# A graph network on one Trainium2 core: the dense sum by source inside the second graph-attention pass, and the residual layer in two stages

## What is computed

```python
x = _layernorm(x + _L0_gnn_ref(x, edge_index, ...))   # two graph-attention passes (gat_conv)
x = _layernorm(x + _L1_gnn_ref(x, src, dst, edge_weight, ...))   # residual layer
x = _layernorm(x + _L2_gnn_ref(x, edge_index, ...))   # attention with queries, keys, values
x = _layernorm(x + _L3_gnn_ref(x, src, dst, ...))     # edge network with batch norms
```

```python
h = (x @ W).reshape(N, H, C)
e = leaky_relu(alpha_s[src] + alpha_d[dst], 0.2)
e_exp = exp(e - segment_max(e, dst)[dst])
alpha = e_exp / (segment_sum(e_exp, dst)[dst] + EPS)
out = segment_sum(h[src] * alpha[:, :, None], dst) + bias

feat_neigh = segment_sum(edge_val[:, None] * feat_in[edge_col], edge_row)
_branch(f, W, b, i): h = relu(f @ W.T + b); (h - mean) * scale_i * rsqrt(var + 1e-9) + offset_i
result = _branch(feat_in, W_self, b_self, 0) + _branch(feat_neigh, W_neigh, b_neigh, 1)
```

## Time and profile before

| what | us |
|---|---|
| three runs | 12797.11, 12800.82, 12800.6 |
| median | 12800.6 |
| profiled execution | 12812.41 |
| its span | 12810.4 |
| busy PE, DVE, ACT, POOL | 3639.8, 6552.3, 2402.6, 7622.7 |
| second pass, first to last unit | 2999 to 5448 |
| from its end to the first copy of the third pass | 5448 to 6644 |

### The profile page before, as it was taken

The page is one execution under the profiler, slowest core; times in us unless marked ns, Lnnn a source line. Parts: engine busy times, 40 slices in busy tenths (PEclk is TensorE's granted clock), DMA queues, the critical chain, the costliest instruction groups (busy, mean ns, idle before and its releaser), DMA issues. The chain is left out here.

```text
span 12810.4 us, 93838 instructions
## 1 busy us (share of the span) xinstructions
PE 3639.8 (28%) x14310; PEld 2391.1 (19%) x14311; DVE 6552.3 (51%) x12405; ACT 2402.6 (19%) x6410; POOL 7622.7 (60%) x7838
## 2 busy tenths in 40 slices
PE   2212223332122233258510000000421111112987
PEld 1102222221012222224310000000221111111433
DVE  6446666664466666630245566665522222223877
ACT  1113233331123333300000000000000000000877
POOL 4667777766767777700047677777057677775013
PEclk7555666655566556679755555555655555555999
DMA  2264434452644444537314644445025533334776
GB/s 58 62 74 94 101 96 106 108 101 60 74 88 100 101 108 108 97 139 260 114 56 111 104 112 112 112 112 104 2 80 96 104 105 104 107 104 113 260 245 222
DMA packets 833811, 1413.84 MB, mean 110 GB/s; under 512 B 184676, under 2 KB 616266, under 8 KB 820952
## 3 DMA queue, kind: packets, MB, share of 16 engines
q0 software_dynamic: 277904, 662.94, 26.2%
q1 hardware_dynamic: 114696, 415.29, 9.4%
q10 hardware_dynamic: 441152, 335.02, 8.9%
HBM read 1057.62 MB, written 355.03 MB: 110 GB/s over the span
## 5 line engine op out<-in xcount | busy, mean ns | idle before, releaser
L818 POOL DMA_INDIRECT ring<-gat_table,index x3640 | 3632.7, 998 | 1229.7 <-issue 1043.2
L818 POOL DMA_INDIRECT ring<-b_table,index x1820 | 1730.4, 951 | 669.8 <-issue 525.8
L818 POOL DMA_INDIRECT ring<-kv_table,index x1820 | 1720.7, 945 | 591.1 <-issue 517.2
L949 PE MATMUL pairs<-hot_lo,hot_hi 128*128 128x128 f32 x6272 | 951.7, 325 | 1377.0 <-ACT hot_lo L979 1375.9
L949 PEld LDWEIGHTS pairs<-hot_lo,hot_hi 128*128 128x128 f32 x6272 | 925.0, 239 | 1430.5 <-issue 1429.0
L979 ACT ACTIVATE hot_lo<-hot_lo,wt 128x128 f32<-128x128 f32 x3136 | 933.9, 387 | 1310.9 <-DMA raw<-in_edges_dram,rid 1140.2
L1628 DVE TENSOR_TENSOR tb<-bt,att 128x1792 f32 x130 | 263.2, 2025 | 1663.6 <-DVEq L106 1663.6
L943 PE MATMUL pairs<-nil 128*128 128x512 bf16 x784 | 389.1, 597 | 2130.8 <-ACT dstage L988 2086.2
L1051 DVE TENSOR_TENSOR first<-ring,p 128x396 f32<-128x396 f32 (+1 forms) x910 | 478.4, 574 | 959.9 <-DVEq L106 953.5
L1650 PE MATMUL bt<-ident,ring 128*128 128x128 f32 x1820 | 416.7, 421 | 1932.2 <-PEq L106 1932.2
L1110 ACT ACTIVATE p<-x 128x56 f32<-128x56 f32 (+1 forms) x390 | 98.2, 252 | 4398.4 <-DVE x L1043 4398.4
(11 more groups left out here) (366 smaller groups left out, 8089.9 us busy)
## 6 DMA issues: line engine op xcount, KB each, us to landing
kept_ring<-kept SPq DMA_DIRECT2D x260, 896.0 KB, 4.6
dense_weights<-dstage ACTq DMA_DIRECT2D x196, 1024.0 KB
mat<-dense_weights SPq DMA_DIRECT2D x98, 1568.0 KB, 6.2
kept<-tb ACTq DMA_DIRECT2D x132, 896.0 KB, 3.8
ring<-gat_table,index POOLq DMA_INDIRECT x3640
ring<-kv_table,index POOLq DMA_INDIRECT x1820
ring<-b_table,index POOLq DMA_INDIRECT x1820
index<-slot_src SPq DMA_DIRECT2D x536, 4.8 KB
```

What stands on the lines that cost most here:

```text
L818: pool.indirect_dma_start(self.ring[:, r * UG + i, :], None, self.table, bass.IndirectOffsetOnAxis(self.index[:, half, at:at + 1], 0)).the ...
L949: mm = pe.matmul(self.ps[:, b, i * P:(i + 1) * P], self.hot_hi[:, 4 * b + i, :], self.hot_lo[:, 4 * b + i, :], start=False, stop=False, sk ...
```

## The change

**Dense rows in two phases.** `PAIRS = 32` becomes `PP = 16`: a tile is built in two phases of 16 pairs, in four PSUM banks instead of eight. DVE marks phase 0 and phase 1 one after the other. ACT fetches, scales and, between the phases, copies and stores phase 0; the store of phase 1 still comes after the tile's exponentials. A store is two DMAs of half the size. Where `take` waited and cleared a semaphore, it is now waited for and lowered.

```diff
+        for u in range(self.PHASES):
+            at = (self.half * self.PHASES + u) * PP
+            part = slice(at, at + PP)
+            with dve.Fori(0, n):
+                dve.wait_ge(self.col_in[u], 32)
+                dve.sem_inc(self.col_in[u], -32)
+                dve.wait_ge(self.used[u], QUADS)
+                dve.sem_inc(self.used[u], -QUADS)
+                c.go(dve.tensor_copy(self.wt[:, u, :], self.col[:, u, 1, part]))
+                c(dve.tensor_copy(self.num[:, 0, :], self.col[:, u, 0, part]))
+                dve.sem_inc(self.col_free[u], 1)
...
+                for b in range(QUADS):
+                    four = slice(4 * b, 4 * b + 4)
+                    ramp = k.ramp[:, :].unsqueeze(1).broadcast_to(shape)
+                    dve.tensor_tensor(self.hot_hi[:, u, four, :], self.hi[:, four].unsqueeze(2).broadcast_to(shape),
+                                      ramp, ALU.is_equal)
+                    dve.tensor_tensor(self.hot_lo[:, u, four, :], self.lo[:, four].unsqueeze(2).broadcast_to(shape),
+                                      ramp, ALU.is_equal).then_inc(self.marked[b], 1)
...
+    def act_phase(self, act, t, u, n):
+
+        row = act.value_load(self.k.chrow[0:1, ds(t, 1)], min_val=1, max_val=EROWS + T)
+        with act.Fori(0, n) as i:
+            act.wait_ge(self.col_free[u], 1)
+            act.sem_inc(self.col_free[u], -1)
+            self.act_fetch(act, u, row + i + 1)
...
+                act.sem_inc(self.marked[b], -1)
+                for j in range(4 * b, 4 * b + 4):
+                    last = act.activation(self.hot_lo[:, u, j, :], self.hot_lo[:, u, j, :], ACT.Copy,
+                                          scale=self.wt[:, u, j:j + 1])
                 last.then_inc(self.built[b], 1)
...
+    def act_store(self, act, t, u):
+
+        act.wait_ge(self.full, 1)
+        act.sem_inc(self.full, -1)
+        act.wait_ge(self.stage_out, 32)
+        act.sem_inc(self.stage_out, -32)
         for b in range(QUADS):
             act.activation(self.stage[:, 4 * b:4 * b + 4, :].rearrange("p i c -> p (i c)"), self.ps[:, b, :],
                            ACT.Copy).then_inc(self.bank_free[b], 1)
         act.drain()
         for x in range(2):
-            act.dma_start(self.cells[ds(t, 1), x, self.half, :, :, :].rearrange("t a i b -> (t a) i b"),
+            act.dma_start(self.cells[ds(t, 1), x, self.half * self.PHASES + u, :, :, :]
+                          .rearrange("t a i b -> (t a) i b"),
                           self.stage[x * CH:(x + 1) * CH, :, :]).then_inc(self.stage_out, 16)
 
     def act_end(self, act):
```

```diff
+    def act_load(self, act, b, w):
+        for u in range(2):
+            act.wait_ge(self.mat_free, 1)
+            act.sem_inc(self.mat_free, -1)
+            at = (2 * w + u) * BLK
+            act.dma_start(self.mat[:, u, :, :], self.view[:, ds(b * B7, B7), at:at + BLK]).then_inc(self.mat_in[u], 16)
+
+    def pe_step(self, pe, w):
+        if w == 0:
+            pe.wait_ge(self.xs_ready, 1)
+            pe.sem_inc(self.xs_ready, -1)
+        for u in range(2):
+            pe.wait_ge(self.mat_in[u], 16)
+            pe.sem_inc(self.mat_in[u], -16)
+            pe.wait_ge(self.ps_free, 1)
+            pe.sem_inc(self.ps_free, -1)
+            for j in range(B7):
+                mm = pe.matmul(self.ps[:, u, 0:BLK], self.xs[:, j, :], self.mat[:, u, j, :], start=(j == 0),
+                               stop=(j == B7 - 1))
+            mm.then_inc(self.done, 1)
+            pe.drain().then_inc(self.mat_free, 1)
+
+    def dve_step(self, dve, w):
+        for u in range(2):
+            dve.wait_ge(self.done, 1)
+            dve.sem_inc(self.done, -1)
+            at = (2 * w + u) * BLK
+            dve.tensor_tensor(self.fnt[:, at:at + BLK], self.ps[:, u, 0:BLK], self.fnt[:, at:at + BLK],
```

```diff
-        p, kept_share = place("p", [P, S, HW]), s.sb("kept_share", [P, HW])
-        first, second = place("first", [P, B7, VB]), s.sb("second", [P, B7, VB])
-        acc = place("acc", [P, B7, VB])
-        step = 3 if beside is not None else B7
+        if VB * B7 + 3 * HW <= 1024:
+            both = s.ps("first", [P, 1024])
+            first = both[:, 0:VB * B7].rearrange("p (w c) -> p w c", w=B7)
+            p = both[:, VB * B7:VB * B7 + (S + 1) * HW].rearrange("p (s c) -> p s c", c=HW)
+        else:
+            first, p = s.ps("first", [P, B7, VB])[:, :, :], s.ps("p", [P, S + 1, HW])[:, :, :]
...
-                    part = slice(at, at + n)
-                    dve.tensor_tensor(acc[:, part, :], acc[:, part, :], second[:, part, :], ALU.add)
+                c(dve.tensor_tensor(by_head(acc[:, :, :]), by_head(acc[:, :, :]),
+                                    weight[:, UG:UG + B7, :].unsqueeze(3).broadcast_to([P, B7, heads, dim + 1]),
+                                    ALU.mult))
+                c(dve.tensor_tensor(first, first, second[:, :, :], ALU.add))
+                dve.tensor_tensor(acc[:, :, :], first, acc[:, :, :], ALU.add)
                 c.reset()
 
-            if rows_of is not None:
-                parts = Running(k, dve, EROWS)
...
+                    for w in range(B7):
+                        rows_of.dve_tile(dve, rows_of.chunks(dve, b * B7 + w))
+                        if before and w:
+                            by_source.dve_step(dve, w - 1)
+                        many = dve.value_load(k.beside[0:1, ds(b * B7 + w, 1)], min_val=1, max_val=UMAX)
                         u = run.value()
                         with dve.Fori(u, u + many) as v:
                             unit(v)
                         run.advance(many)
+                if before:
+                    by_source.dve_step(dve, B7 - 1)
                 c(dve.drain())
 
...
                 c(dve.tensor_scalar(rden[:, :], a4[:, :, dim], 1e-16, None, ALU.add))
                 c(dve.reciprocal(rden[:, :], rden[:, :]))
-                c(dve.tensor_tensor(k.out[:, ds(b * B7, B7), :].rearrange("p w (h c) -> p (w h) c", h=heads),
...
+                    act.wait_ge(e_ready, 1)
+                    act.sem_clear(e_ready)
+                    act.activation(p, x[:, :, :], ACT.Exp)
 
                     act.activation(e[:, S, :], newmax[:, :], ACT.Copy).then_inc(p_ready, 1)
+
+            def band(b, before):
+                for w in range(B7):
+                    t = b * B7 + w
+                    if before:
+                        if w == 0:
+                            act.wait_ge(rows_of.stage_out, 32)
+                        by_source.act_load(act, b - 1, w)
+                    n = rows_of.chunks(act, t)
+                    for u in range(rows_of.PHASES):
+                        rows_of.act_phase(act, t, u, n)
+                        if u < rows_of.PHASES - 1:
+                            rows_of.act_store(act, t, u)
+                    exponents(act.value_load(k.beside[0:1, ds(t, 1)], min_val=1, max_val=UMAX))
...
                 rows_of.act_end(act)
-
-
-
```

```diff
+            c.until(seen)
+            c.go(dve.tensor_tensor(var[:, :], st6[:, :, 2], st6[:, :, 5], ALU.add))
+            c.go(dve.tensor_tensor(mid[:, :], st6[:, :, 1], st6[:, :, 4], ALU.add))
+            c(dve.tensor_tensor(dif[:, :], st6[:, :, 1], st6[:, :, 4], ALU.subtract))
+            c(dve.scalar_tensor_tensor(dif[:, :], dif[:, :], 0.25, dif[:, :], ALU.mult, ALU.mult))
+            c(dve.scalar_tensor_tensor(var[:, :], var[:, :], 1.0 / D, dif[:, :], ALU.mult, ALU.add))
+            inverse_root(dve, c, var, dif, seed, 1e-5)
+            c(dve.scalar_tensor_tensor(mid[:, :], mid[:, :], -0.5, var[:, :], ALU.mult, ALU.mult))
+            for w in range(B7):
+                put = c.go(dve.tensor_scalar(o[:, w, :], o[:, w, :], var[:, w:w + 1], mid[:, w:w + 1], ALU.mult,
+                                             ALU.add))
+            c.until(put)
+            dve.sem_inc(by_source.xs_ready, 1)
+            c(dve.tensor_copy(skip[:, ds(t, B7), :], o))
 
         attention_pass(k, table, slot_src, VB + H, H, C, scores, start, finish, extra,
```

```diff
-        add_rows(k, k.out[:, :, :], k.out[:, :, :], x)
-        layernorm(k, k.out[:, :, :], x, 1e-5)
-        residual_layer(k, x, a["L1_gnn_W_self"], a["L1_gnn_b_self"], a["L1_gnn_W_neigh"], a["L1_gnn_b_neigh"],
-                       a["L1_gnn_scale"], a["L1_gnn_offset"], dense, by_node)
...
+        both_branches(k, x, fnt, (ws, wn), br, own, own_std, own_mid, by_node, kv)
+        join_branches(k, x, own, own_std, own_mid, sc, of, shift, by_node, (wv, wk, wq), qb, table, kv)
...
+            base(0)
+            for b in range(NB):
+                join(b)
+                if b + 1 < NB:
+                    base(b + 1)
+                queries(b)
```

601 lines of the change are left out of this document (375 added, 226 removed).

## The result

The changed kernel takes 12164.8 us (median of four runs, 12145.3 to 12168.4) where the kernel before took 12800.7: a ratio of 0.950, interval 0.9486 to 0.9514. That is 636 us less; the forecast was 12071 us, 730 less, in a range from 11860 to 12260. The profiled execution has a span of 12166.3 us, 644 less than before.

What follows compares the result with a forecast made beforehand. POOL's indirect copies were taken to pace the passes, with 1196 us of serial stages between two of them; 12810 - 813 (serial stretch) - 80 (pass 1) + 164 (pass 2) = 12081 us span, median 12071, range 11860 to 12260.

Steps and rivals of the forecast that it cites:

- the serial stretch: Between the second pass and the next: 1196 us of dense sum and short stages shrink to 383, giving 813 us.
- Tail: Last band's dense sum left over behind pass 2: 14 loads and 14 product groups, 95 us with the start.
- both branches with weights: Stage of both branches behind the sum, 85 us (bounds 70 and 119), plus 16 for weights, blocks and one memset.
- join: Stage before the next pass, DVE's row operations with row gathers run ahead: 187 us, bounds 150 and 230.
- the term said to decide: Pass 2: matrix loads ahead of the fetch on ACT's queue make two-unit tiles 44 us; the pass costs 164 more.
- held fetch: ACT's phase-0 fetch in pass 2, let go when the first load has gone, 16.6 us after the copies began.
- The first step of that working: Pass 2: ACT's second load waits for PE's sums of the tile before; at the low clock 5 us a tile.
- rival D: Matrix loads of 1792-byte pieces hit few memory banks and take 30 us; slower than before, 13000 us; chance 0.03.
- Even: Pass 1: a two-unit tile takes 35.2 us and POOL needs 35.1, so the pass keeps its 80 us gain.
- A: Rival for pass 2: the queue swallows the loads, tiles stay at 36 us, POOL sets the pace: 11867; chance 0.20.
- B: Rival: loads of 9 to 13 us or PE at 1.2 GHz, tiles 47 to 52 us: 12160 to 12480; chance 0.20.
- C: Rival: copies from gat_table stay at 998 ns, so pass 1 keeps its time: 12151 us; chance 0.06.

Runs made afterwards that it cites:

- e1: Changed kernel with the 84 matrix loads inside the second pass left out, products and additions kept: 11983.4 us.
- e2: Changed kernel with all matrix loads moved behind the second phase's scalings, ahead of the exponentials, and the wait for the band's last store dropped: 11987.8 us.
- e6: Changed kernel with the two matrix loads of a tile placed right behind the first phase's fetch, ahead of its scalings: 12038.0 us.
- e12: Changed kernel with PE doing a tile's two groups of the sum between its two phases of pairs, loads still ahead of the fetch: 12157.9 us.

## Why the prediction was right, and where it was off

The span was forecast at 12081 us and is 12166, 85 more: pass 1 and what lies before it gave 35 us less than forecast, pass 2 took 67 more, the serial stretch 19 less, the rest 2 more.

**The serial stretch** was forecast at 383 us and is 364. That it is so close is luck in part, since its pieces are off in both directions. Tail 108 for 95, both branches with weights 73 for 101, join 183 for 187. The tail's step is 6.9 us where 6.3 were assumed (12.6 for two), and its first group begins 12 us after the last unit. Both branches take 64 us without the weights, under the lower bound of 70: DVE's 12 us a band were far too high, it goes from one band to the next in 5.3 us, two additions and two groups of statistics.

**Pass 2** was the term said to decide. The held fetch was forecast at 16.6 us after the copies and measured at 14.5, a middle tile of two units at 44 and measured at 43.9 (19 tiles, 835 us for 836), one of three units at 51 and measured at 50.5. So the mechanism held, and the match of the tile is luck in part. In the tile shown the fetch goes 2.1 us earlier than forecast, but phase 0's copies begin 3.1 us after the scalings where 1.3 were put down for PE, so they end at 24.7 us, where 24.8 were forecast. And 18 of the 19 tiles take 43.1 us on average; the last of them, near the end of band 6, takes 59.7, and 41.3 with the empty slots spread. That the hold comes from the queue, and not from bytes or from PE, is what e1, e2, e6 and e12 show together. The first step of that working, that PE's sums come late enough to matter only at the low clock, had the right outcome for another reason: the wait is there at the high level of the clock too (5.50 us for 14 instructions, granted clock 1.00 in that stretch, 4831 to 4837), covered by the hold.

The 67 us by which pass 2 is longer than forecast lie in two kinds of tiles; the other tiles come out 6 us under. A first tile of a band was put at 55 and takes 59.7 (28 us over six): the missing step is the jump back over DVE's long program, and with the short loop it takes 54.8. A last tile was put at 51 and takes 58.6 (46 us over six): the missing step is that its units' gathers read one row again and again, which slows the store, the loads and the fetch; with spread slots it takes 49.5. It takes both, though: with the sum's loads gone and the slots as they were (e1), it takes 49.2. The hot stretch of band 0 was in the trace, and rival D named it, but as a sign of what the matrix loads might do. I did not ask what caused it, nor that it recurs at the end of every band.

**Pass 1** was forecast to give 80 us and gives 45. The copies did what was said, 998 to 954 ns. The step that failed is "Even": first exponential at 27.5 us and a tile of 35.2. They are 30.1 and 37.7 on average. The terms as listed add up to 28.0, not 27.5, and the second fetch and what stands around it were put too low by 2 us: it is let go at 24.8 us in the like tile of pass 1 above, where 27.5 less the scaling of 4.7 is 22.8. POOL needs 35.1 for two units, and so the last bands hang on ACT; a stretch of slow reads at the pass's end then holds the fetch 9 us.

**The rivals.** A, that the queue swallows the loads: not so ahead of the fetch, but nearly so behind the scalings. B, slow loads or a low clock: the sign named for it, loads landing after 9 us or more, did appear, 14.8 us, and pass 2 at +231 is near its lower edge of +250. But the same loads land in 8.8 us when they stand behind the fetches (e2), and the tail's step is 6.9 us, so it is their place in the queue; and 5.50 us for the 14 instructions of a group, in 97 of the 98 groups, rules out the low clock. C, copies that stay at 998: no. D, loads of 30 us: no; a step of 6.9 us in the tail against 614/98 = 6.3 of the old stage is the most that pieces of 1792 bytes can have cost there.

## What to carry to other kernels

A small transfer that an engine waits for belongs ahead of the large ones on its queue (another queue for it was not tried): the sum inside the pass cost 236 us with its loads ahead of the fetch, and 47 with them behind the scalings (1911 us for bands 1 to 6, against 1864 without a sum). Give padding its own rows, many of them: one row read by all empty slots made each packet take six times as long, 0.76 us instead of 0.12, and the kernel with more transfers on ACT's queue lost more by it, 303 us against 149. Where an operation beside a descriptor-making POOL has both inputs in SBUF, put one in PSUM; where that cannot be, cutting the operation softens it (a copy took 1.34 us beside cut ones, 1.66 to 1.76 beside whole ones, 0.94 with one input in PSUM).

## What the runs showed that was not expected

The loop over the bands cost DVE about 3.5 us on each of six returns in the first pass and 6.2 us on each of five in the second once its seven tiles were unrolled, and 0.7 us with the short loop. Two waits that stand one behind the other on ACT did not add: taking the wait for PE away (e12) changed nothing, and taking the loads away left 2.1 us of a middle tile over pass 1's 37.7. And moving two loads of 1568 KB by some 24 us within the tile gave back 189 of the 236 us.
